# The first K projection's passes over high parts ahead, unit 0's low parts behind its four sums

## The reference, cut to what matters

```python
x = x + attn(cond(x, cond_128, ...), w_attn, w_proj, adapter_wte, gating)
x = x + ffn(cond2(x, cond_128, ...), W_base, ...)

# cond: a mixing matrix for each of the 32 batches, chosen by a small MLP with a softmax
out = einsum('boi,bih->boh', agg_w, x) + agg_b[:, :, None]     # x is (32, 64, 1024)
# attn: 32 heads of 32, rotary embedding, causal over 64 rows, and 10 adapter rows
qkv = einsum('btc,oc->bto', out, w_attn)
```

## Time and profile before

| | us |
|---|---|
| median of 3 runs | 1141.3 (1140.57 to 1144.7) |
| span of the profiled execution, first to last instruction | 1139.1 |
| TensorE busy in it | 1132.2 |
| VectorE busy in it | 923.4 |
| ScalarE busy in it | 359.6 |

### The profile page before, as it was taken

One profiled execution on the slowest core, in us unless ns is written; L12 is line 12 of the kernel. 1 busy time (PEld: TensorE's weight loads), 2 busy tenths in 40 slices (PEclk: granted clock), 3 DMA queues, 4 the chain that ended last, 5 costly groups with the idle time before them and its releaser, 6 DMA issues.

```text
span 1139.1 us, 21477 instructions
## 1 busy us (share of the span) xinstructions
PE 1132.2 (99%) x8632; PEld 950.7 (83%) x8632; DVE 923.4 (81%) x1740; ACT 359.6 (32%) x665; POOL 54.1 (5%) x24
## 2 busy tenths in 40 slices
PE   9999999999999999999999999999999999999998
PEld 6888888888888888888888888878888888888887
DVE  5999879879889789798798799888767777877765
ACT  5433333333342432433433334323222211122210
POOL 0000000000000000000000000110000022221112
PEclk9999999999999999999999999999999999999999
DMA  6515115114125034034033177885549933233312
GB/s 222 182 56 167 67 34 162 66 53 153 56 75 167 20 97 155 12 106 146 20 111 130 45 270 269 322 251 164 185 129 347 345 89 104 96 116 116 98 38 93
DMA packets 99701, 151.81 MB, mean 133 GB/s; under 512 B 7443, under 2 KB 84115, under 8 KB 96915
## 3 DMA queue, kind: packets, MB, share of 16 engines
q1 hardware_dynamic: 98594, 135.76, 36.5%
q10 hardware_dynamic: 1008, 14.68, 3.1%
HBM read 95.88 MB, written 54.54 MB: 132 GB/s over the span
## 4 chain that ended last, share of the span: by engine, by line
PE 92%; DVE 4%; DMA 2%; issue 1%; ACT 0%; SPq 0%; DVEq 0%; ACTq 0%
PE psum L948 44%; PE psum L1026 23%; PE psum L1044 5%; PE psum L931 3%; PE psum L916 2%; PE psum L900 2%; PE psum L1078 2%; PE psum L1060 2%; PE psum L276 2%; DMA y_scratch<-a_ysb 2%; PE psum L960 2%; PE psum L909 1%; PE psum L1062 1%; PE psum L972 1%; PE psum L230 1%
## 5 line engine op out<-in xcount | busy, mean ns | idle before, releaser
L948 PE MATMUL psum<-z,w_hi 128*128 128x512 f32 x1536 | 481.5, 395 | 0.2 <-DVE z L374 0.2
L948 PEld LDWEIGHTS psum<-z,w_hi 128*128 128x128 f32 x1536 | 282.5, 188 | 57.2 <-DVE z L374 0.4
L948 PE MATMUL psum<-z,w_lo 128*128 128x512 f32 x768 | 300.5, 391 | 0.0
L1026 PE MATMUL psum<-f_wform,f_act_hi 128*128 128x512 f32 (+1 forms) x912 | 279.9, 389 | 1.3 <-DVE f_u L1494 1.1
L1026 PEld LDWEIGHTS psum<-f_wform,f_act_hi 128*128 128x128 f32 x912 | 167.9, 188 | 35.8 <-issue 2.6
L1026 PE MATMUL psum<-f_wform,f_act_lo 128*128 128x512 f32 (+1 forms) x456 | 176.2, 386 | 0.0
L948 PEld LDWEIGHTS psum<-z,w_lo 128*128 128x128 f32 x768 | 144.1, 188 | 30.6
L1026 PEld LDWEIGHTS psum<-f_wform,f_act_lo 128*128 128x128 f32 x456 | 85.7, 188 | 17.4
L875 POOL TENSOR_TENSOR f_xn<-f_x,_bbase 128x1024 f32<-128x1024 f32 x16 | 50.5, 3158 | 1009.0 <-DVE f_x L1520 678.5
L1218 ACT ACTIVATE f_act_hi<-f_act_sum 128x512 fp32r<-128x512 f32 x64 | 40.3, 632 | 119.2 <-DVE f_act_sum L1469 48.1
L1218 ACT ACTIVATE f_act_hi<-f_raw 128x512 fp32r<-128x512 f32 x56 | 33.7, 626 | 102.7 <-DVE f_raw L1552 64.8
(11 more groups left out here) (173 smaller groups left out, 1491.7 us busy)
## 6 DMA issues: line engine op xcount, KB each, us to landing
w_forms<-f_prep_lo SPq DMA_DIRECT2D x16, 896.0 KB, 5.2
f_wform<-w_forms SPq DMA_DIRECT2D x7, 2048.0 KB, 13.2
f_wform<-w_forms ACTq DMA_DIRECT2D x7, 2048.0 KB, 16.9
w_st<-in_wqkvT SPq DMA_DIRECT2D x7, 1536.0 KB, 6.3
w_forms<-f_prep_hi SPq DMA_DIRECT2D x16, 640.0 KB, 6.2
m_x<-in_x SPq DMA_DIRECT2D x16, 512.0 KB, 5.5
y_scratch<-a_ysb SPq DMA_DIRECT2D x32, 256.0 KB, 2.8
f_raw<-y_scratch SPq DMA_DIRECT2D x8, 1024.0 KB, 6.0
```

What stands on the lines that cost most here:

```text
L948: mm = pe.matmul(dst, w[:, c, x, :], zs, start=(c == 0 and i == 0), stop=(c == KC - 1 and i == 2))
L1026: mm = pe.matmul((prod_bank[i], bank[0])[part][:, cols], a[:, c, :], wform[i][:, w, c, cols], start=(i < 4 and c == 0 and n == 0), stop=(c ...
```

## The change

K's first projection is taken apart. First come, for all eight chunks, the two passes over the high part of z (high weights and low weights), behind a wait for the four high parts (`z_hi`) alone. Then, behind the wait for the four low parts (`z_lo`), the eight passes of the high weights over the low part. One mix stands behind each fourth chunk of these, so two in all; the next ones follow in Q and V by the old rule (behind each second chunk, while there are any). On VectorE the four sums of unit 0 come first, and its four low parts behind them; sum 4 follows. Nothing else of the lists changes.

```diff
--- before.py
+++ after.py
@@ -376,7 +376,7 @@
     def clear(pool):
         pool.memset(aggT[:], 0.0).then_inc(cleared, 1)
 
-    return (Sync, clear, Tensor, Scalar, Vector), ctx_out, z_mm, z_sum, z_lo
+    return (Sync, clear, Tensor, Scalar, Vector), ctx_out, z_mm, z_sum, z_hi, z_lo
 
 
 def program(nc, d, psum, z, zbase, y_dram, x1_dram, w_forms, ctx_dram, aggb_dram, weights, out):
@@ -591,7 +591,7 @@
 
             return t.manual_sbuf_range[0]
 
-        parts, ctx_out, z_mm, z_sum, z_lo = mixing(
+        parts, ctx_out, z_mm, z_sum, z_hi, z_lo = mixing(
             nc, ctx, d, psum, z, z[:, :, :, :, :].bitcast(F32),
             [Space(nc, "f", zbase + u * Z + Z // 2).take(f"z_raw{u}", [P, KC, UT]) for u in range(NU)], ctx_dram, aggb_dram,
             (wst, whi, wlo, whi_f, w_first, w_hi, w_lo),
@@ -1083,9 +1083,21 @@
                 AHEAD = UP + 2
                 for i in range(AHEAD):
                     mix_tensor.mix(pe, i)
+                pe.wait_ge(w_lo[K_], 1)
+                pe.wait_ge(z_hi, UP)
+                for c in range(KC):
+                    for n, w in enumerate((whi, wlo)):
+                        pe.matmul(bK, w[:, c, K_, :], z[:, 0, 0, c, :], start=(c == 0 and n == 0), stop=False)
                 pe.wait_ge(z_lo, UP)
                 i = AHEAD
-                for x, dst in ((K_, bK), (Q_, bQ), (V_, bV)):
+                for c in range(KC):
+                    mm = pe.matmul(bK, whi[:, c, K_, :], z[:, 0, 1, c, :], start=False, stop=(c == KC - 1))
+                    if c == KC - 1:
+                        mm.then_inc(mm_done[K_], 1)
+                    if c % 4 == 3:
+                        mix_tensor.mix(pe, i)
+                        i += 1
+                for x, dst in ((Q_, bQ), (V_, bV)):
                     for c in range(KC):
                         project_chunk(x, dst, 0, 0, c)
                         if c % 2 and i < NP:
@@ -1338,11 +1350,10 @@
         @block.vector
         def _(dve):
             mix_vector.begin(dve)
-            mix_vector.add(dve, 0)
-            for i in range(1, UP):
+            for i in range(UP):
                 mix_vector.add(dve, i)
-                mix_vector.low(dve, i - 1)
-            mix_vector.low(dve, UP - 1)
+            for i in range(UP):
+                mix_vector.low(dve, i)
             mix_vector.add(dve, UP)
 
             def mix_on(i0, i1):
```

## The result

| | before | after |
|---|---|---|
| median of 5 runs | 1141.3 us | 1149.3 us (1148.19 to 1150.59) |
| ratio, 95% interval | | 1.0071 [1.0058, 1.0083] |
| span of the profiled execution | 1139.1 | 1147.5 |

What follows compares the result with a forecast made beforehand. TensorE was taken to bound the kernel, busy 1132.2 of 1139.1 us. K's start -1.0, K to mix 13 -0.4, and mix 13 to mix 14 +6.7 gave +5.3 on 1141.3: 1146.6 us, range 1143.2 to 1149.5.

Steps and rivals of the forecast that it cites:

- The front: Opening mixes up to K: sums 2 and 3 no longer behind low parts, so K starts 1.0 us earlier.
- the landing of x for mix 5: Ahead of K: x lands at 24.64, so mix 5 starts at 24.75; 24.25 if the landing does not hold it.
- K is fed: In K's split passes: high parts there 1.4 us early, low parts 1.7 us early, so no wait.
- The first stall: In V ahead of the adapter's turn (L938): PE waits 3.05 us for ScalarE's copy akv, behind sum 13 and high 13.
- The second stall and the late sum: Ahead of unit 1's scores: PE waits some 3.5 us, as VectorE's sum 15 starts at 67.8, 5.3 us later.
- rival 2: At the adapter's turn: akv comes in time, only the late rotation counts; +2.1 us, 1143.4; chance 0.06.
- The clock: TensorE behind both stalls: no fall to the lower clock counted in the forecast's own sum, as no row showed one.
- Rival 1: TensorE behind the stalls: the clock falls, some 3 us each; one fall 1149.6, both 1152.6; chance 0.10.
- a sign that it was wrong: On PE behind a stall: passes above 600 ns would show the prediction wrong.
- its own case: Whole kernel: both stalls without a fall of the clock, +5.3 us, 1146.6; likeliest range 1145.3 to 1148.0; chance 0.76.

Runs made afterwards that it cites:

- e5: Changed kernel with ScalarE's copy akv ahead of high parts 12 and 13, and 15 unused products in the second stall only: 1144.50 us, ratio 1.0023.
- e4: Changed kernel with 12 and 15 unused products of a constant tile put in the two stalls: 1147.65 us, ratio 1.0050.
- e2: Kernel before with only the mixes' places changed: two in K, four in Q, four in V: 1151.42 us, ratio 1.0088.
- e3: Changed kernel with ScalarE's copy akv moved ahead of the high parts 12 and 13: 1145.57 us, ratio 1.0036.
- e6: Kernel before with VectorE's new list alone (four sums, then four low parts): 1142.39 us, ratio 1.0012.
- e7: Changed kernel with four mixes in K and VectorE's list of before: 1141.35 us, ratio 1.0011.

## Why the forecast was right in direction and 2.7 us short

- *The front.* Forecast -1.0, measured -1.32. The term that was off is the landing of x for mix 5: it did not hold mix 5 in the profiled run, and held it by 0.86 in e5. It belongs in the bounds, where it was.
- *K is fed.* z_lo came 1.4 us ahead of its use (low parts done at 28.2, first low pass at 29.64), forecast 1.7. Right.
- *The first stall.* Forecast 3.05 us and on akv, measured 2.88 as a wait and 3.15 as its part of the way (e4 less e5). Right.
- *The second stall and the late sum.* Forecast 3.5, measured 3.46. Right. Sum 15 is late by 3.1 from K on (rival 2's own +2.1 is this 3.1 less the 1.0 at the front); e5 shows it.
- *The clock.* This is the step that failed: "Against it: PE is partly busy throughout, and the short gaps seen so far did nothing", with a chance of 0.10. Rival 1 is what happened, in both stalls, with passes of 0.63 us where the prediction had named passes above 600 ns behind a stall as a sign that it was wrong. The clock fell in all four traces with an unfilled stall of over 2 us (changed, e2, e3, e6). The rule of the Trainium skill, "TensorE: Matmul & The Clock Gate", section "Why this matters for your kernels", against idle gaps between bursts, spoke for it. These traces agree, with two gaps (2.88 and 2.35 us) shorter than those it warns of; by the mean clocks of e6's executions, most of them had no fall behind the shortest. Rival 1's price was sized in two equal parts of 3 us. The first cost 2.8, since six passes and mix 14, all on the way to sum 14, ran slow. The second cost 0.75 in this trace, since few passes ran before the clock rose; behind the same wait it cost 1.15 in e3 (20.68 less e5's 19.53) and 2.3 in e2.
- *Together.* -1.32 + 3.1 + 3.15 + 2.8 + 0.75 = +8.5, where the spans differ by 8.4. The four prices from K on add up to the table's stretches by construction, since each is a difference between neighbours in the series before, e5, e4, changed. Without the falls it is +4.9, and the forecast's sum was +5.3. The clock is more than the whole of the miss in size.
- That the range held the result at its upper edge (1149.3 under 1149.5) is in part luck: its own case held no fall, rival 1 had 1149.6 for one and 1152.6 for both, and both came but cost 3.5 us, not 6. A slowdown beyond 0.5% had 0.42, less than the 0.56 for no change. With more weight on the clock's case that order would have been the other way.

## What to carry to other kernels

Whoever splits a loop in two and thins out what was interleaved in it moves all the interleaved work behind it. Look for the first place where a moved piece now stands right ahead of a wait that another engine's written order ties to that piece; here it was worth 3 us, and restoring the density in the loop kept the gain without it.

A stall of TensorE can be priced twice: the wait, and the work behind it at half the clock. How much the second part is depends on what runs while the clock is low, and on how long that is, which differs between executions. If a new idle gap is longer than any in the trace of before, the absence of falls in that trace is no evidence.

## What the runs showed of the hardware

- In the profiled executions gaps of 2.88 and 3.46 us on TensorE, and one of 2.35 in e6, came with a granted clock near 0.5. In the changed kernel it fell within the first stall (57 to 58 us read 0.76, the stall ends at 58.31), and was low for some 6 us behind the first stall and some 3 behind the second. In e2, with the same two waits, it fell about 1 us behind the first stall's end (59 to 60 us read 1.00, 60 to 64 us 0.59), and 71 to 77 us read 0.50. So both the moment of the fall and the time spent low differ for like gaps.
- A like gap does not always have its fall. Eight of e6's ten executions have a mean granted clock of 1.000. That each of them had its gap of some 2.35 us is likely, as they ran the same program, but only one was profiled.
- With products of a constant in both gaps (e4), or in the second with the first gone (e5), the clock reads 1.00 in all executions.
- The opening differs between executions of kernels whose lists are the same up to the sixth mix. In e6 the six mixes took 13.86 us and began at 16.57; in the changed kernel they took 11.19 and began at 14.94. So the six mixes end 4.3 us later in e6. The long opening stands in the profiled executions of e3, e4 and e6. The 25 runs of the kernel before that stood beside e5 to e7 fall into two groups, 1139.3 to 1141.8 (20 runs) and 1144.9 to 1145.1 (5 runs). That the clock's rise in the opening makes these two groups was not tried, only read off the lengths of the same instructions.
- The medians of e3, e4 and e5 stand 1 to 2 us above what their stretches add up to. The opening and a late x for mix 5 can make up such an amount, and in e3 a longer fall as well (a mean clock of 0.997 in three of its eight executions, 0.998 or 0.999 in the others); what share each has stays open.
